# A second attention stage rewritten as a straight list of eight-head slots, with the two halves of TensorE's rows alternating

## What is computed

```
Q = (layernorm(x) @ Wq) * mask;  K = (ctx @ Wk) * mask;  V = (ctx @ Wv) * mask     # per head, 64 features
scores = Q K^T / 8;  attn = softmax(scores) * mask;  attn = attn / sum(attn)
x = x + concat(attn V) @ Wo
```

## Time and profile before

| | |
|---|---|
| median of 3 executions | 1665.94 us (1664.78 to 1668.11) |
| the profiled execution: its own time | 1669.45 us |
| its span, first to last instruction | 1667.7 us |
| mean granted TensorE clock over the span | 0.877 of full |
| first attention, from its first maxima to its end | about 72 to 312 us of the span |
| second attention, from the end of its weights | about 893 to 1476 us of the span |

### The profile page before, as it was taken

One profiled execution on the slowest core, in us unless ns is written; L12 is line 12 of the kernel. 1 busy time (PEld: TensorE's weight loads), 2 busy tenths in 40 slices (PEclk: granted clock), 3 DMA queues, 4 the chain that ended last, 5 costly groups with the idle time before them and its releaser, 6 DMA issues. The chain is left out here.

```text
span 1667.7 us, 30058 instructions
## 1 busy us (share of the span) xinstructions
PE 1351.9 (81%) x10824; PEld 1082.2 (65%) x10824; DVE 959.2 (58%) x2070; ACT 810.0 (49%) x1334; POOL 662.6 (40%) x556
## 2 busy tenths in 40 slices
PE   2578787343999999999993798898988989836798
PEld 1366665242788888888871577787777777726586
DVE  3455644256565556565553676765666666436665
ACT  1266666321444444444442475664755657521454
POOL 1376756220455555555550123322333233311254
PEclk9987977555999999999996799998999999965799
DMA  4121120410000000000001000000000000010000
GB/s 125 61 66 53 48 67 5 106 47 0 1 1 0 1 1 1 0 0 0 0 0 63 0 2 1 2 2 3 2 2 3 2 1 2 2 32 1 1 26 25
DMA packets 29697, 31.43 MB, mean 19 GB/s; under 512 B 6197, under 2 KB 24162, under 8 KB 29442
## 3 DMA queue, kind: packets, MB, share of 16 engines
q1 hardware_dynamic: 28546, 29.57, 6.0%
q10 hardware_dynamic: 1024, 0.13, 0.0%
HBM read 23.16 MB, written 6.29 MB: 18 GB/s over the span
## 5 line engine op out<-in xcount | busy, mean ns | idle before, releaser
L1411 POOL TENSOR_TENSOR w_lo_f<-weighted_f,w_hi_f 128x512 fp32r<-128x512 f32 x232 | 300.9, 1297 | 346.5 <-ACT w_hi_f L1353 346.5
L565 POOL TENSOR_TENSOR p_lo_l<-probs_l,p_hi_l 128x512 f16<-128x512 f32 x128 | 148.4, 1159 | 338.5 <-ACT p_hi_l L358 338.5
L1391 DVE TENSOR_TENSOR hidden_f<-psum,gate_act_f 128x512 f32<-128x512 f32 x232 | 160.5, 692 | 210.6 <-PE psum L1303 199.8
L1368 ACT ACTIVATE gate_act_f<-psum 128x512 f32<-128x512 f32 x232 | 138.7, 598 | 269.7 <-PE psum L1303 268.4
L988 POOL TENSOR_TENSOR p_lo_a<-probs_a,p_hi_a 128x1024 f16<-128x1024 f32 x64 | 136.3, 2129 | 87.8 <-ACT p_hi_a L847 87.6
L1397 DVE TENSOR_TENSOR weighted_f<-psum,hidden_f 128x512 f32<-128x512 f32 x232 | 160.5, 692 | 9.0
L1303 PE MATMUL psum<-x_lo_f,w_hi 128*128 (+1 forms) x384 | 153.6, 400 | 0.0
L1301 PE MATMUL psum<-x_hi_f,w_hi 128*128 (+1 forms) x384 | 152.1, 396 | 1.8 <-PEq L1199 1.8
L1302 PE MATMUL psum<-x_hi_f,w_lo 128*128 (+1 forms) x384 | 151.9, 395 | 0.0
L1353 ACT ACTIVATE w_hi_f<-weighted_f 128x512 fp32r<-128x512 f32 x232 | 144.6, 623 | 2.2 <-DVE weighted_f L1397 2.2
L356 ACT ACTIVATE probs_l<-psum,lift_l 128x512 f32<-128x512 f32 x128 | 88.0, 688 | 106.5 <-PE psum L232 106.5
(11 more groups left out here) (257 smaller groups left out, 3657.2 us busy)
## 6 DMA issues: line engine op xcount, KB each, us to landing
q_pad_a<-narrow_q SPq DMA_DIRECT2D x64, 64.0 KB
k_x_a<-narrow_k SPq DMA_DIRECT2D x24, 128.0 KB
narrow_q<-q_hl_a SPq DMA_DIRECT2D x8, 256.0 KB, 2.0
narrow_k<-k_hl_a SPq DMA_DIRECT2D x8, 256.0 KB, 2.0
out<-x_all SPq DMA_DIRECT2D x8, 256.0 KB, 2.3
pick_raw<-c_pick SPq DMA_DIRECT2D x1, 1536.0 KB, 6.2
k_x_a<-narrow_k SPq DMA_DIRECT2D x8, 124.0 KB
stage<-L_ffn_w SPq DMA_DIRECT2D x3, 256.0 KB, 2.9
```

The costliest lines, as they stand in the source:

```text
L565: nc.gpsimd.tensor_tensor(p_lo[:, r, :], probs[:, r, :], p_hi[:, r, :], ALU.subtract).then_inc(s_exp_lo, 1)
L1368: nc.scalar.activation(gate_act[:, slot, :], GATE[slot][:, :], ACT.Silu).then_inc(s_silu, 1)
L1391: nc.vector.tensor_tensor(hidden[:, slot, :], UP[slot][:, :], gate_act[:, slot, :], ALU.mult).then_inc(s_hid, 1)
L1411: nc.gpsimd.tensor_tensor(w_lo[:, slot, :], weighted[:, (parity * nc_ + k) % 2, :], w_hi[:, slot, :].bitcast(F32), ALU.subtract).then_inc( ...
```

## The change

`attention(...)`, `Attn` and their loop are removed. `attention1` does the same work:

- A slot is half a batch: eight heads, 1024 columns of scores in one pair of banks (only one pair). There are 64 slots in a straight list, without a loop.
- In scores and maxima, matmuls go in turn to rows 0 to 63 and rows 64 to 127: `part` is the inner loop. The two halves write to different banks.
- Fills, transposed maxima, transposed att and output share a ring of three banks (`RING1`), in the order that `work1(s)` gives: up to three items ahead of scores(s+1) ("head"), the others between values(s-1, 0) and values(s-1, 1) ("tail").
- Values of a slot are two halves of four heads, each with its own wait on `p_lo`, which GpSimd forms in two halves of 512 columns.
- Exponentials are 1024 columns long. The factor 64 is added to the transposed maxima in place of a bias of the exponential.
- Statistics of a group come 13 slots ahead of its first slot, and its normalisation moves from VectorE to GpSimd. The copy of the mask (L559) is dropped.

No DMA is added, removed or moved. The core of the diff:

```diff
-            attention(nc, scope, 1, bank, x_all, ctx_all, const, w)
+            attention1(nc, scope, psum, x_all, ctx_all, const, w)
...
+    table = {0: (1, "k0 k1", ""), 1: (1, "q2 k2", "q3 k3"), 2: (1, "q4 k4", ""), 3: (1, "q5 k5", "q6 k6"),
+             4: (1, "q7 k7", ""), 5: (1, "v0 v1", "v2 v3"), 6: (1, "v4 v5", ""), 7: (1, "v6 v7", "")}
+    group = s // 8 + 1
+    head += fills(group, table[rel][1])
+    tail += fills(group, table[rel][2])
+    if rel == 6:
+        tail += fills(s // 8 + 2, "x")
+    if rel == 7:
+        tail += fills(s // 8 + 2, "c q0 q1")
+    if s % 2 == 0 and 0 <= s - 4 < 2 * B:
+        head.append(("out", (s - 4) // 2))
+    if s % 2 == 0 and 0 <= s + 2 < 2 * B:
+        tail.append(("nmt", (s + 2) // 2))
+    if 0 <= s - 2 < 2 * B:
+        tail.append(("att", s - 2))
+    return head[:3], head[3:] + tail
...
+            def scores(s):
+                b, j = divmod(s, 2)
+                tok, par = slice(b % GB * P, (b % GB + 1) * P), b // GB % 2
+                await_free(("nmt", b))
+                if s:
+                    pe.wait_ge(s_exp_hi, s)
+                for i in range(4):
+                    ch = 4 * j + i
+                    for hi_q, hi_k in ((True, True), (False, True), (True, False)):
+                        for part in range(2):
+                            rows = slice(64 * part, 64 * part + 64)
+                            k = (k_a if hi_k else k_b)[rows, par, ch, tok]
+                            q = (q_a if hi_q else q_b)[rows, par, ch, tok]
+                            nc.tensor.matmul(T_BANK[:, part, i * P:(i + 1) * P], k, q, start=hi_q and hi_k, stop=False)
+                    for part in range(2):
+                        rows = slice(64 * part, 64 * part + 64)
+                        last_ = nc.tensor.matmul(T_BANK[:, part, i * P:(i + 1) * P], sel[rows, ch, :],
+                                                 negmax_t[rows, b % 2, :], start=False, stop=True)
+                last_.then_inc(s_sc, 1)
...
+            def values(s, part):
+                pe.wait_ge(s_plo, 2 * s + part + 1)
+                ...
+                if 2 * s + part:
+                    pe.wait_ge(s_att, 2 * s + part)
...
+            def shared(item):
+                if count:
+                    pe.wait_ge(s_free[bank], count)
...
+            for s in range(FIRST, LAST):
+                head, tail = work1(s)
+                for item in head:
+                    shared(item)
+                if 0 <= s + 1 < NP:
+                    scores(s + 1)
+                if 0 <= s + LM1 < NP:
+                    maxima(s + LM1)
+                if 0 <= s - 1 < NP:
+                    values(s - 1, 0)
+                for item in tail:
+                    shared(item)
+                if 0 <= s - 1 < NP:
+                    values(s - 1, 1)
...
+            def exponentials(s):
+                act.wait_ge(s_sc, s + 1)
+                if s >= 2:
+                    act.wait_ge(s_plo, 2 * (s - 2) + 2)
+                if s >= 3:
+                    act.wait_ge(s_pv, 2 * (s - 3) + 2)
+                pair = T_BANK.rearrange("p a n -> p (a n)")
+                nc.scalar.activation(probs[:, s % 2, :], pair, ACT.Exp, scale=scale)
+                nc.scalar.activation(p_hi[:, s % 3, :], pair, ACT.Exp, scale=scale).then_inc(s_exp_hi, 1)
...
+                    for part in range(2):
+                        half = slice(512 * part, 512 * part + 512)
+                        nc.gpsimd.tensor_tensor(p_lo[:, s % 3, half], probs[:, s % 2, half], p_hi[:, s % 3, half],
+                                                ALU.subtract).then_inc(s_plo, 1)
```

More of the change, by code:

```diff
@@ L21 @@
 G = B // GB
[L22 to L26, removed]
 EPS = 1e-5
@@ L33 @@
 NONE = -1e30
[L36 to L65, removed]
@@ L989, in _, with work1, fills @@
                                             ALU.subtract).then_inc(s_plo, 1)
+RING1 = 3
+LM1 = 4
+def work1(s):
+    head, tail = [], []
+    rel = s % 8
+    g = (s + 10) // 8
+    def fills(group, names):
+        return [(n[0], (group, int(n[1:] or 0))) for n in names.split()] if 0 <= group < G else []
+    table = {0: (1, "k0 k1", ""), 1: (1, "q2 k2", "q3 k3"), 2: (1, "q4 k4", ""), 3: (1, "q5 k5", "q6 k6"),
[14 more added lines that the diff above has]
+    return head[:3], head[3:] + tail
```

735 lines of the change are left out of this document (282 added, 453 removed).

## The result

The changed kernel takes 1540.23 us in the median of four runs (1538.84 to 1540.95); the kernel before took 1665.84 (1664.78 to 1668.11) beside it. The ratio is 0.924, with a 95% interval of 0.923 to 0.926: 125.6 us less, where 91 were forecast. The profiled execution took 1538.84 in its own time, with a span of 1537.0. The forecast had the sign, and the overlap of the two halves came as forecast; the time lies 35 us under it, and 5 under the lower end of the range.

What follows compares the result with a forecast made beforehand. It took TensorE, or what stops it, to bound the second attention. Start 935, seven groups of 57, last group 45 and end 6 gave 1385 against 1476: 91 less, so 1575 us, range 1545 to 1632.

Steps and rivals of the forecast that it cites:

- the overlap of the two halves: Scores and maxima: matmuls on different row halves run at the same time; 32 scores take 1.28 us a slot, not 2.24.
- VectorE's part of the walk: Slot-by-slot chain: second values wait for VectorE's division, next head's fills for its remainders; odd slot 7.8 us, even 5.55.
- I add 4% for the spread that strict queues bring: Margin on the walked time of a group of eight slots, raising it from 55 to 57 us.
- the sum of the dense unit: Old kernel's second attention: TensorE's pieces in one dense unit sum to 3.11 us, 2% under the 3.17 in the row.
- I take the lower end: Price of each score matmul with halves in turn: 0.032 us rather than 0.056, making TensorE's work 47 us per eight slots.
- No overlap: Rival: score matmuls keep the 0.056 pitch, a group takes 64.5 us, 35 less in all, 1631; chance 0.17.
- The clock falls in the gaps: Rival: TensorE's clock drops partly, to 0.79, in the new slots' gaps; group 63 us, time 1617; chance 0.17.
- The low clock: Rival: clock stays low in the second attention; 0.78 takes the whole gain, 0.67 gives 1688 to 1736; chance 0.06.
- It does not do what it says: Case that the halved wait on `p_lo` brings nothing; already counted in the forecast, without a chance of its own.
- The signs: Listed trace signs: score pairs under 0.056 apart, stage under 460 us, odd slots about 2 us longer, no edge, GpSimd never awaited.

Runs made afterwards that it cites:

- The halves-apart kernel: The changed kernel with scores and maxima going through all of rows 0 to 63, then all of rows 64 to 127, same banks: 1583.16 us, ratio 0.950.

## Why the prediction was wrong in its size and right in its kind

**The sum against the trace.** The forecast had the first scores at 935, seven groups of 57, the last group and the end 51: 1385. In the profile (starts in TensorE's timeline) the first scores start at 929.6, those of the second group at 978.0 and of the last at 1292.6; the last addition ends at 1345.8. So the start is 5 early; the first group, whose queues are still filling, takes 48 instead of 57 (9); six groups take 52.45 instead of 57 (27); and the end takes 53 instead of 51: 39 in all. The two profiles stand 3.6 above and 1.4 below their medians, which leaves the 35 that the medians show.

**The step that failed: VectorE's part of the walk ("only then may TensorE do the second values", "their banks are what the next head's two fills wait for"), and "I add 4% for the spread that strict queues bring".** TensorE's own work was right: 47 per group, measured 47.7. What came on top was forecast as 8 of waits (55) and 2 of spread (57), and measured 4.8. Odd slot, counted from its scores at 1149.35, walked and then measured:

- VectorE free of the head's remainders: 1.5, measured 1.34.
- reduction done, first division begins: 2.75, measured 2.48.
- first division done: 3.6, measured 3.30 (1152.65); the second remainder that follows: 5.05, measured 4.60 (1153.95).
- TensorE's transposes of att done, second values begin: 3.6 and 3.65, measured 3.52 for both.
- next head's fills begin: 4.4 and 5.15, measured 3.96 and 4.76.
- last fill done: 5.85, measured 5.47; next scores: 7.8, measured 7.34.

Every piece on VectorE was a duration, and behind a remainder or the reduction the next instruction starts 0.07 to 0.09 us before such a duration is over. Piece by piece that adds up: the queue is 0.30 early at the first division's end and 0.45 at the second remainder's. With that the two waits of the walk vanish. The second values follow TensorE's own transposes and not the division; the second fill follows the first and not the remainder. Without waits, the walk's own pieces give 3.6 + 0.4 + 1.4 + 1.85 + 0.1 = 7.35, and the slot takes 7.34: the odd slot is TensorE's work, where the forecast had it as VectorE's chain. The even slot does wait for the division, as walked, and is 5.38 instead of 5.55. A pair is 0.63 shorter, four pairs 2.5. Slots 6 and 7 add 1.6, as walked. The other 2.0 are the 4% that I added for spread: five of the six groups in the middle of the stage take 52.44 to 52.51 us and the last one 52.29, since every queue is a fixed list and the waits fall in the same places. 2.5 + 2.0 is the whole 4.55 of the group. The 2% by which the sum of the dense unit was low justified no margin on a sum of durations, which errs to the high side.

The Trainium skill, ScalarE: Activation LUTs (What ACT_TABLE_LOAD costs), states that back-to-back ACTIVATEs overlap by about 93 ns; the trace agrees, with two copies of 0.60 in 1.11 (1142.76) and an exponential of 1.02 followed after 0.90 (1146.84 to 1147.74). The Trainium skill, VectorE: DVE Perf Modes (Two Vector instructions with no wait between them), tells of instructions that are not held and start before earlier ones have finished; the remainders and the reduction here do.

**"I take the lower end"** (0.032 for each score matmul) was right and was not low enough: it measured 0.028, so the pair costs what one did. The halves-apart kernel gives 43 us for 12 of 20 pitches, so some 72 for the whole by the estimate above; the forecast without overlap, 1631 against 1575, had given it 56. That upper case would then be some 1612, so it too came out high, with the same pieces of VectorE and the same 4% in it. The Trainium skill, TensorE: Matmul & The Clock Gate (Part 3, Packing small matmuls), was right against the rows alone. The trace agrees with its 4 ns too: in 915 of the 1024 pairs of score matmuls the second starts 3 or 4 ns behind the first.

**The rivals.** No overlap: excluded by the pitch. The clock falls in the gaps: it stayed at 1.00 in the two groups, with TensorE busy 91% of the time and standing still for 1.1 us at a time. Only in the last group, which has no fills, was it at half for two stretches of 3.4 us, among waits of up to 1.4 us. The low clock: nothing of it. The evidence that the prediction named for both was misread: it put the three slices at 0.5 of the earlier trace rows in the first attention, but they reach from 292 to 417 us, and that attention ends at 312. "It does not do what it says" held for the halved wait, as forecast.

**The signs** came as listed: pairs closer than 0.056 per matmul, a stage of 416 us, an odd slot 1.96 longer than an even one, no edge, GpSimd scarcely waited for. Two came in part. Second values wait for the division in even slots only. The next head's fills hardly wait for the tail's remainders: the first starts 0.06 us behind the end of its remainder (1153.25 and 1153.31), some 0.08 later than it could, and the second not at all.

**Where the 126 us came from.** At the end of the stage the two profiles differ by 130.6 us (5 of it is how far they stand from their medians). 8.0 lie before the first scores, 1.4 of them before this attention's first instruction. The 122.5 in the stage are all TensorE's busy time, at an idle time of 50 us in either kernel. Three terms make up most of them:

- The overlap: 20 pitches of 0.056 in each of 64 slots, 72 us. A run shows 43 of it, the rest is the estimate above.
- The clock. In the kernel before, TensorE's clock was granted at half in eight stretches of the stage, one of them and their sum here; in the changed kernel in the two of the last group. TensorE was busy in 73.75 us of them before and in 6.1 now. What it did there would have taken half the time at the full clock: 34 us.
- Changes of form: one pair of changes less for two units, 0.2 in 64 slots, 13 us. This is an estimate from the earlier trace rows.

```profile
1145.40:1159.00 13.60, 12.73 (x108) 11.27 (x109) 7.28 (x22) 5.59 (x9) 6.38 (x9) 0.50 0.01 3
...
sum 81.30, PE 73.75 PEld 64.53 DVE 39.88 ACT 33.42 POOL 24.19; mean PE 9.22 PEld 8.07 DVE 4.99 ACT 4.18 POOL 3.02
```

```profile
1304.20:1307.60 3.40, 2.93 (x44) 2.36 (x38) 1.90 (x4) 0.69 (x2) 1.49 (x2) 0.50 0.02 5
1314.50:1317.90 3.40, 3.17 (x54) 3.00 (x55) 0.94 (x2) 0.09 (x1) 2.27 (x2) 0.51 0.02 5
```

That is 119 of 122.5. What the clock's part is worth by itself no run shows. Six of the eight stretches at half clock come once in a step of the old list, one of them is that of the earlier trace rows; but taking loop and normalisation out of the old order did not bring it back.

## What to carry to other kernels

For a chain through one engine's queue, sum start-to-start distances of instructions that follow one another without a wait, not durations, and add no margin for spread where all queues are fixed lists: repeat one period exactly. Walk each kind of slot by itself: which engine ends it can differ from slot to slot, and an average over the stage hides that. Here VectorE ends the even slots and TensorE the odd ones, so a us added to VectorE cost 0.87, while 0.19 us less in each of four divisions brought 0.19 in a pair of slots. Small matmuls that use only half of the rows are worth alternating between the halves when both halves have their own bank, since the second then cost nothing here. To price such an overlap by a run without it, look at the trace of that run: the order of the list alone did not take all of it away. Before moving an output or a fill, follow the ring bank that it needs: the same edit brought 4 us with a bank in the way and 9 without.

## What the runs showed of the hardware

- Two matmuls of 64 rows by 128 columns (float16) on different halves start as a pair every 0.056 us, the pitch of one alone. The second starts 3 or 4 ns behind the first in 915 of 1024 pairs.
- With the halves one after the other, four matmuls at the end of one half still run in pairs with the first four of the other, so a matmul later in the list starts ahead of earlier ones (1156.68 ahead of 1156.73, above): 32 pitches for 40 matmuls instead of 20, and 0.68 us more a slot.
- Back-to-back pitch against length: VectorE 0.60 against 0.69 (remainder), 1.14 against 1.21 (reduction); ScalarE 0.90 against 1.02 (exponential of 1024).
- The granted clock stayed at 1.00 in the windows of two whole groups, with TensorE busy in 91% of them and its longest wait 1.1 us. In the kernel before it fell behind stops of several us. In the changed kernel's last group it fell to 0.50 for 3.4 us, twice. With the normalisation on GpSimd it was 0.72 in two windows in which TensorE was busy for 4.90 and 5.35 of 6 us; what drew it down there I did not find.
